# Two items of the next batch moved later in an attention loop: a key item to between the passes, a query item into the second pass

## The reference

```python
h = concat([ctx, x], axis=1)                      # 512 rows
q = (x @ q_w + q_b).reshape(b, 256, 16, 32)
k, v = split(h @ kv_w + kv_b)                     # 512 rows each
attn = where(mask, q @ k.T / 32, -inf)            # per head, 256 x 512
out = softmax(attn) @ v
out = out @ out_w + out_b + x
out = rmsnorm(out) ; out = gelu(out @ w1 + b1) @ w2 + b2 + x
```

## Time and profile before

| | us |
|---|---|
| median of 3 runs | 2311.32 |
| the profiled execution | 2312.23 |
| its span, first to last instruction | 2310.4 |
| PE busy | 2278.0 |
| ACT busy | 1432.6 |
| DVE busy | 1063.7 |
| POOL busy | 420.0 |
| one iteration of layer 0's loop | 58.8 |

### The profile page before, as it was taken

The page is one execution under the profiler, slowest core; times in us unless marked ns, Lnnn a source line. Parts: engine busy times, 40 slices in busy tenths (PEclk is TensorE's granted clock), DMA queues, the critical chain, the costliest instruction groups (busy, mean ns, idle before and its releaser), DMA issues.

```text
span 2310.4 us, 42833 instructions
## 1 busy us (share of the span) xinstructions
PE 2278.0 (99%) x14366; PEld 1873.6 (81%) x14366; DVE 1063.7 (46%) x1942; ACT 1432.6 (62%) x3378; POOL 420.0 (18%) x522
## 2 busy tenths in 40 slices
PE   9999999999999999899999999999999999999998
PEld 7777888888888887688888888888888888888886
DVE  7555555555555555532112112112165655656563
ACT  5777777777777777643222222222257878787786
POOL 4222222222222223300000000001022121211110
PEclk9999999999999999899999999999999999999998
DMA  7444444444444444341011011012055555655553
GB/s 216 112 120 119 118 112 112 117 119 119 119 119 119 119 118 99 101 146 55 1 54 54 0 54 54 0 54 91 1 166 135 149 140 140 148 136 152 130 130 89
DMA packets 141971, 239.12 MB, mean 103 GB/s; under 512 B 25393, under 2 KB 59601, under 8 KB 139873
## 3 DMA queue, kind: packets, MB, share of 16 engines
q1 hardware_dynamic: 140512, 238.05, 38.9%
q10 hardware_dynamic: 1408, 0.41, 0.1%
HBM read 86.28 MB, written 25.21 MB: 48 GB/s over the span
## 4 chain that ended last, share of the span: by engine, by line
PE 54%; ACT 1%; DVE 1%; DMA 1%; SPq 0%; issue 0%; DVEq 0%
PE item_ps L66 7%; PE item_ps L68 6%; PE item_ps L67 6%; PE score_ps L67 5%; PE score_ps L66 5%; PE score_ps L68 5%; PE o_ps L66 4%; PE o_ps L68 4%; PE o_ps L67 4%; PE score_ps L1435 3%; PE score_ps L1408 3%; PE o_ps L1451 2%; PE item_ps L1289 1%; ACT score_ps L850 1%; SPq L535 0%; DMA layer_result<-rows 0%
## 5 line engine op out<-in xcount | busy, mean ns | idle before, releaser
L850 ACT ACTIVATE score_ps<-score_ps,l_neg_max 128x512 f32<-128x512 f32 (+1 forms) x1024 | 566.3, 556 | 187.1 <-DVE l_neg_max L1094 183.1
L1094 DVE TENSOR_REDUCE l_neg_max<-score_ps 128x1 f32<-128x512 f32 (+1 forms) x768 | 496.9, 684 | 97.4 <-PE score_ps L1408 95.2
L1884 ACT ACTIVATE mlp_hidden<-score_ps,b_col 128x512 f32<-128x512 f32 x128 | 88.2, 689 | 498.7 <-PE score_ps L68 453.8
L1932 DVE TENSOR_TENSOR mlp_hidden_l<-mlp_hidden,mlp_hidden_h 128x512 fp32r<-128x512 f32 x128 | 92.9, 726 | 513.5 <-ACT mlp_hidden_h L1886 513.4
L66 PE MATMUL item_ps<-feats_h,weights_l 128*128 128x256 f32 (+1 forms) x1024 | 323.5, 316 | 2.7 <-POOL feats_l L705 1.1
L67 PE MATMUL item_ps<-feats_l,weights_h 128*128 128x256 f32 (+1 forms) x1024 | 317.2, 310 | 0.0
L68 PE MATMUL item_ps<-feats_h,weights_h 128*128 128x256 f32 (+1 forms) x1024 | 316.9, 309 | 0.0
L1408 PE MATMUL score_ps<-l_stack 97*128 97x512 f32 (+1 forms) x1024 | 295.0, 353 | 7.0 <-DMA l_stack<-l_qk 3.1
L870 ACT ACTIVATE l_probs<-score_ps 128x1024 f32<-128x1024 f32 x272 | 269.2, 1024 | 33.1 <-PE score_ps L1435 26.9
L1435 PE MATMUL score_ps<-l_stack 99*128 99x256 f32 x1536 | 249.1, 292 | 2.7 <-ACT score_ps L850 1.1
L1435 PEld LDWEIGHTS score_ps<-l_stack 99*128 99x128 f32 x1536 | 214.2, 192 | 46.1 <-issue 29.2
(11 more groups left out here) (165 smaller groups left out, 4032.1 us busy)
## 6 DMA issues: line engine op xcount, KB each, us to landing
l_stack<-room SPq DMA_DIRECT2D x254, 192.0 KB, 3.2
l_stack<-l_qk SPq DMA_DIRECT2D x254, 128.0 KB, 2.4
l_stack<-room SPq DMA_DIRECT2D x130, 128.0 KB, 2.9
l_tokens<-in_features SPq DMA_DIRECT2D x16, 1024.0 KB, 4.8
l_stack<-l_qk SPq DMA_DIRECT2D x254, 64.0 KB, 2.1
l_stack<-room SPq DMA_DIRECT2D x130, 64.0 KB, 3.0
l_rows<-in_x SPq DMA_DIRECT2D x16, 512.0 KB, 3.3
norm_transposed<-norm_room SPq DMA_DIRECT2D x16, 512.0 KB, 2.7
```

The source lines that it names most:

```text
L850: m = act.activation(e, e, ACT.Exp, bias=neg_max[:, q, h:h + 1], accum_out=row_sum[:, q, h:h + 1])
L1094: dve.tensor_reduce(out, bank, AXIS_X, ALU.max, negate=True).then_inc(max_done, 1)
L1884: act.activation(hidden[:, m % HBUF, :], hidden_ps[:, m % 4, :], ACT.Gelu_apprx_tanh, bias=b1_col[:, m:m + 1])
L1932: dve.tensor_tensor(hidden_p[1][:, m % HBUF, :], hidden[:, m % HBUF, :], f32(hidden_p[0][:, m % HBUF, :]), ALU.subtract).then_inc(hidden_l ...
```

## The change

`MIXED` goes from 5 to 4: slot "item 4" goes away, key 3 (item 4) is computed between the passes, and query 1 (item 5) in the second pass, in group 1 where the first projection stood. `high(p, 5)` stands behind `exps(5)` on ACT, `low(p, 5)` between `o_low(0)` and `o_low(1)` on DVE. Group g projects group g - 2, and the projection of group 2 comes behind the last group, before the four scores ahead. The 28 steps are spread over nine slots: late 2, late 3 and item 1 hold one more each, item 3 one less. In the last batch (no `p`) there is no item in group 1, only the projections are later.

```diff
-    MIXED = 5 if first else NT + NK - 1
+    MIXED = 4 if first else NT + NK - 1
...
-    STEPS_AT_FIRST = [2, 3, 3, 2, 2, 3, 3, 3, 3, 2] if first else [2, 2, 2, 2, 2, 2, 2, 2]
-    STEPS_IN_SLOT = [3, 3, 3, 2, 2, 4, 3, 3, 3, 2] if first else [1, 1, 1, 1, 0, 3, 3, 2]
+    STEPS_AT_FIRST = [3, 3, 3, 2, 2, 4, 3, 3, 3] if first else [2, 2, 2, 2, 2, 2, 2, 2]
+    STEPS_IN_SLOT = [3, 3, 3, 3, 3, 4, 4, 3, 2] if first else [1, 1, 1, 1, 0, 3, 3, 2]
...
                     for s in range(KB * (g + 1), KB * (g + 2)):
                         exps(a, s)
+                        if p is not None and s == KB + 1:
+                            high(p, MIXED + 1)
...
                     o_low(a, 0)
+                    if p is not None:
+                        low(p, MIXED + 1)
                     o_low(a, 1)
...
-                    if g == 1:
-                        items_free(p)
-                    project_tile(a, g - 1, 0)
+                    if g == 1 and p is not None:
+                        item(p, a, MIXED + 1)
+                    elif g > 1:
+                        if g == 2:
+                            items_free(p)
+                        project_tile(a, g - 2, 0)
                     shifted(a, KB * g + 2)
-                    project_tile(a, g - 1, 1)
+                    if g > 1:
+                        project_tile(a, g - 2, 1)
                     shifted(a, KB * g + 3)
                     run(g)
+                project(a, FB - 2)
```

## The result

The changed kernel takes 2316.93 us (median of 12 runs), the kernel before 2310.64 us beside it (12 runs): ratio 1.0028, 95% interval 1.0020 to 1.0036. It is 6.3 us slower (4.6 to 8.3). Forecast was 2314.5 us, which is +3.2 us.

A forecast was written before the change was run, and what follows sets the result against it. PE bounds the kernel, busy 2278.0 of 2310.4 us. 14 x (0.46 + 0.04) + 0.1 - 4.3, with 0.03 each at `shifted` 2, made +3.2 us: 2315.4 profiled, 2314.5 as median; range 2305.5 to 2322.

The forecast's parts named there:

- group 1: Second pass: `high(p, 5)` holds exps 6 and 7 on ACT, PE waits 0.59 us before the last `weigh`; +0.27 us.
- last batch: Layer 0's last batch: PE no longer waits for the first `o_low`, group 2 begins earlier; together -4.3 us.
- groups 2 and 3: Second pass: no wait for `o_low`, part given back at the third `shifted` waiting for exps 8; -0.25 us an iteration.
- boundary: Between the passes, key item replaces query item: similar PE time, nothing late; second pass's +0.02 becomes +0.04 us with it.
- first pass: Loses one item but keeps all 28 steps, so PE waits at two tight places; +0.46 us an iteration.
- step 19: First pass: its score comes before ACT ends the sum of step 15 that it needs; +0.11 us.
- `shifted` 2: At the boundary: waits for exps 0 by 0.1 us as now; 0.03 us an iteration added to the sum.
- Step 28: First pass: DVE's chain without a hole makes its score wait for the sum of step 24; 0.33 us.
- A: Rival: the first pass hides its steps, -3.6 us, 2307.7 us; chance 0.24.
- B: Rival: DVE and ACT bound the first pass's end, in its last slot; +11.9 us, 2323 us; chance 0.14.
- D: Rival: ACT, not `o_low`, sets the groups, late projections only uncover exps 8; +0.25 us x 14 more, 2318 us; chance 0.12.
- C: Rival: by the shared-port rule DVE's shift ends 0.9 us later in the first pass; +15 us, 2327 us; chance 0.04.

The follow-up runs named there:

- e3: Changed kernel with `high(p, 5)` on ACT behind exps 7 in place of exps 5: 2315.40 us, ratio 1.0012 against the kernel before.
- e5: Changed kernel with group 1's query item cut in quarters around `shifted` 6 and 7, and `high(p, 5)` behind exps 7: 2310.48 us, ratio 0.9993 against before.
- e6: The cut alone: changed kernel with group 1's query item cut in quarters, `high(p, 5)` left behind exps 5: 2330.45 us, ratio 1.0081 against before.
- e7: Changed kernel with one of the 28 steps taken from slot late 3 and put into v 0: 2313.00 us, ratio 1.0004 against before.
- e1: Kernel before with projections one group later only in the last batch, no item moved: 2308.53 us, ratio 0.9986 against before.
- e4: Changed kernel with one step less in slot late 3, one more in the query's slot: 2315.46 us, ratio 1.0011 against before.
- e2: Kernel before with projections one group later in every batch, items unmoved, nothing filling group 1: 2321.58 us, ratio 1.0042 against before.

## Why the prediction was right, and where it was off

The time lies inside the range and the mechanism was the forecast one, a gain in the last batch and a larger loss in the loop; but the forecast was a change within 0.2%, and the measured +0.28% is beyond that. By its steps (us in an iteration, but for the last row):

| step | forecast | measured | from |
|---|---|---|---|
| group 1 | +0.27 | +0.22 | 7.41 - 5.69 + 1.38 - 2.88 |
| groups 2 and 3 | -0.25 | -0.09 | 11.11 against 11.20 |
| boundary | +0.02 | +0.09 | 6.24 both, with three quarters of an item 0.09 us shorter |
| first pass | +0.46 | +0.35 | hole at step 19 |
| iteration | +0.53 | +0.61 | 59.46 less 58.85 |
| last batch | -4.3 | -4.7 | 28.38 against 33.06 |

The four terms of the iteration add to +0.57 as measured; 0.04 us of the +0.61 stand in none of them. The forecast's +0.53 has 0.03 us at `shifted` 2 besides its terms.

- **Group 1** was right in place, order and size: the `high` in front of exps 6 and 7, which e3, e5 and e6 confirm one by one. That a part of the loss lies in PE's own order is seen only once the `high` is moved.
- **Groups 2 and 3** are the mis-sized term. The step "PE goes on at T+1.85: of the 0.24 us won, 0.10 to 0.12 us are given back" had the wait right (0.11 us) and left out what stands behind a wait: the next matmul took 0.10 us more. I had read just that at the projection's first matmul, counted it as won there, and not charged it where the new wait stands.
- **The first pass** came out near the forecast by luck, by two errors that cancel. Step 19 waited about the 0.11 us forecast, but it cost 0.35. Step 28 was to wait 0.33 us and waits for nothing. The failed link is DVE's shift: it took 1.05 us in the changed kernel (231.32 to 232.37) against the 1.41 us taken from the earlier trace rows. The rest of the chain was right: from the max of step 17 (225.93) to that of step 24 (233.04) pass 7.11 us, where 7.46 were forecast. In e7 the shift takes 1.22 us and PE comes without the hole at step 19, but score 17 stands ahead of two products there and its max is off the chain; from the max of step 18 (225.43) to that of step 24 (232.10) pass 6.67 us, just what the forecast's links give with this shift, and the sum is out 0.1 us before PE needs it.
- **The last batch** was right. e1 has it alone. The granted clock of 0.51 in the earlier trace rows followed the 2.53 us wait; in e1, which has no such wait, it is 1.00 from 953.5 to 958.8.
- **Rivals.** A (no first-pass wait) is what e7 makes of the change, but e7 comes to +1.5 us and not to A's -3.6: groups 2 and 3 and the boundary keep 0.2 us an iteration that A gave away. B's place, the last slot, shows clearly in e4 alone (0.12 us). D was half right: ACT sets the groups' third `shifted`. C, the port rule, would have made it +15 us; the subtraction of the first shift did not stand to the end of POOL's instruction.
- **The remainder.** Layer 0 ends 5.05 us later in the profile, where +3.2 was forecast: the iterations have 1.1 us more than forecast, the last batch 0.4 less, and 1.1 us lie outside of both. For these the sum had only the +0.1 of the first iteration: PE reaches the second turn of the last batch 9.73 us later, and 14 iterations make 8.5. Of these 1.2 us, 0.5 are the longer wait for the last batch's first shift (3.65 us, 3.14 before); the rest was not traced. The last instruction comes 7.0 us later. The matmuls behind layer 0 are the same in all ten kernels, and the time from the last batch's turn of the norm to the last matmul is between 1321.6 and 1324.8 us in their profiles. The 1.9 us added there lie within this spread; what sets it was not tried.

## What to carry to other kernels

Work moved to fill a hole on the busiest engine brings its copy-out along, and that stands in the queue of another engine: put it behind what the busy engine waits for next, and only then choose the order on the busy engine (the cut alone cost 0.95 us an iteration against the changed kernel; on top of the moved copy it won 0.33). Count a wait on PE as its length plus what the next one or two matmuls lose, here 0.1 to 0.25 us: several waits of a tenth of a microsecond are worth as much as one that the list of waits shows. Look for them in PEld's row, where the waiting weight load has its idle time. When a slot loses work, the steps must be spread anew by where the partner engines have room, not evenly.

## What the runs showed of the hardware that was not expected

- A wait that PE's list of waits does not show (0.12 us) cost 0.35 us on PE (e7 against the changed kernel), and the waits of 0.11 us before the third `shifted` another 0.10 us each.
- The second shift of DVE met POOL's two additions. DVE, then POOL, in order of time in the changed kernel:

```profile
243.14 0.55 DVE L1103 TENSOR_TENSOR l_log_sum<-l_neg_max,l_log_sum 128x16 f32<-128x16 f32 x1 [1.09 <-ACT l_log_sum L855]
243.72 1.22 DVE L1105 CAST l_shift<-l_log_sum 128x16 fp32r<-128x16 f32 x1
```

```profile
242.37 2.54 POOL L765 TENSOR_TENSOR l_rows<-l_rows,l_bo 128x512 f32<-128x512 f32 x2 [9.49 <-DMA l_rows<-in_x]
```

The CAST, 0.17 us at the median of the earlier trace rows, ends at 244.94, 0.03 us after POOL's second addition; the operation before it ends at 243.69, about where POOL's first one does (its second starts at 243.62). Here DVE did stand to the end of POOL's instruction. That is the rule of the Trainium skill ("SBUF — State Buffer", section "SBUF: two separate sides"). It cost nothing, since PE needs this shift only at 246.46.
- The first shift followed that rule in part, more than the prediction read in the earlier trace rows. Two of POOL's instructions, each shown by itself, and a CAST, all in the kernel before:

```profile
229.22 1.56 POOL L745 TENSOR_SCALAR l_rows<-l_rows,l_stat 128x512 f32<-128x512 f32 x1
934.49 1.56 POOL L114 TENSOR_SCALAR weights_h<-room,norm_w 128x512 fp32r<-128x512 f32 x1
935.38 0.17 DVE L1103 CAST l_shift<-l_log_sum 128x16 fp32r<-128x16 f32 x1
```

The slow CAST of the earlier trace rows ends at 229.27, just behind the start of POOL's second TENSOR_SCALAR; in e7 it ends at 230.85, with that start at 230.80. So it stood to the end of the first one. But the subtraction behind it ends at 229.93, well before POOL does, and the whole shift of the last batch ran in 0.50 us within one TENSOR_SCALAR. What decides when DVE is held was not tried.
- With exps whose scores are all ready, ACT's four exps took 3.80 us from the first's start to the last's end (e2, 252.44), against 4.18 and 4.09 us in the earlier trace rows. In the first of these the third and fourth exps start at 251.67 and 252.84, 0.03 and 0.04 us after their scores' last matmul; in e2 the four starts are 0.92 to 0.93 us apart.
